# A fused attention and expert kernel: four engines in a new order, LayerNorm's shift on GpSimd, TensorE's program without a loop

## The reference, cut to what matters

```python
# x, ctx: (32, 128, 1024) float32. For each of 32 batches:
a  = layernorm(x, axis=-1)
q  = Wq @ a + bq;  k = Wk @ ctx + bk;  v = Wv @ ctx + bv       # 128 x 1024 each
k, v = pad(k, 8, 7), pad(v, 8, 7)
attn = softmax over a window of 16 keys around each position, 8 heads of 16 channels
x1 = x + Wo @ (attn weights times v) + bo
z  = layernorm(x1, axis=-1)                                   # 128 rows of 1024
w  = softmax(z @ gate_w.T); the top 2 of 8 experts, weights normalised to sum 1
out = x1 + sum over experts e of w[:, e] * ((z @ lora_A[e].T) @ lora_B[e].T)   # rank 64
```

## Time and profile before

| | |
|---|---|
| median of 3 runs | 1264.25 us (1264.19 to 1271.45) |
| the profiled execution | 1263.59 us, of which 1261.8 us are its span |
| PE busy | 1074.9 us, 85% of the span, 24452 matmuls |
| DVE / ACT / POOL busy | 898.5 / 574.4 / 416.9 us |
| mean granted clock of TensorE | 0.916 of full speed |

### The profile page before, as it was taken

One profiled execution on the slowest core, in us unless ns is written; L12 is line 12 of the kernel. 1 busy time (PEld: TensorE's weight loads), 2 busy tenths in 40 slices (PEclk: granted clock), 3 DMA queues, 4 the chain that ended last, 5 costly groups with the idle time before them and its releaser, 6 DMA issues.

```text
span 1261.8 us, 55007 instructions
## 1 busy us (share of the span) xinstructions
PE 1074.9 (85%) x24452; PEld 909.8 (72%) x24452; DVE 898.5 (71%) x1922; ACT 574.4 (46%) x809; POOL 416.9 (33%) x306
## 2 busy tenths in 40 slices
PE   4658898988989888998988989888988888989986
PEld 2547786776778677776776878677876777877875
DVE  3567777776768767777776778777677776778873
ACT  4545535444545444444444444444454444455431
POOL 3563323333323233233333223233233333323220
PEclk8778998889989889988989989989988989989999
DMA  4422233123232123232123232123231232332210
GB/s 169 121 70 53 70 87 80 47 67 87 70 86 72 51 70 86 71 86 66 57 70 87 70 87 66 59 67 87 71 86 42 64 86 71 87 86 69 55 36 34
DMA packets 157313, 92.87 MB, mean 74 GB/s; under 512 B 139680, under 2 KB 139808, under 8 KB 156704
## 3 DMA queue, kind: packets, MB, share of 16 engines
q1 hardware_dynamic: 157088, 89.25, 25.4%
HBM read 55.16 MB, written 16.78 MB: 57 GB/s over the span
## 4 chain that ended last, share of the span: by engine, by line
issue 43%; POOL 20%; PE 16%; DVE 13%; ACT 4%; DMA 2%; SPq 1%; POOLq 0%; DVEq 0%
PE bank_a L310 8%; POOL prob L911 8%; POOL ctx_split L917 5%; PE bank_c L310 3%; POOL x_split L943 3%; PE bank_b L360 3%; POOL attn_split L934 2%; DVE row_max L744 2%; DVE row_sum L758 1%; PE bank_b L339 1%; DMA raw<-x 1%; ACT k_sb L575 1%; DVE prob L750 1%; SPq L246 1%; DVE stats L673 1%
## 5 line engine op out<-in xcount | busy, mean ns | idle before, releaser
L911 POOL TENSOR_TENSOR prob<-prob,row_inv 128x512 f32<-128x512 f32 x128 | 134.4, 1050 | 427.8 <-DVE row_inv L762 426.1
L360 PEld LDWEIGHTS bank_b<-prob_t,v_diag 64*64 64x64 f32 x4608 | 214.3, 148 | 49.2 <-issue 26.2
L360 PE MATMUL bank_b<-prob_t,v_diag 64*64 64x96 f32 (+2 forms) x4608 | 228.8, 257 | 15.4 <-DMA v_diag<-v_t 14.4
L310 PE MATMUL bank_a<-down_split,mid_split 128*128 128x264 f32 (+1 forms) x1536 | 215.9, 289 | 8.5 <-issue 6.8
L310 PEld LDWEIGHTS bank_a<-down_split,mid_split 128*128 128x128 f32 x1536 | 194.8, 189 | 16.5 <-issue 8.6
L769 DVE STREAM_TRANSPOSE prob_t<-prob 128x768 f32<-128x768 f32 x128 | 124.9, 976 | 111.8 <-POOL prob L911 110.6
L310 PE MATMUL bank_a<-up_split,ht_split 128*128 128x512 f32 x768 | 194.3, 402 | 3.5 <-DVE ht_split L859 3.5
L558 ACT ACTIVATE prob<-prob 128x512 f32<-128x512 f32 x128 | 80.8, 631 | 248.5 <-DVE prob L750 248.3
L339 PEld LDWEIGHTS bank_b<-k_sb,q_diag 32*32 32x32 f32 x16384 | 153.4, 104 | 39.5 <-issue 33.3
L339 PE MATMUL bank_b<-k_sb,q_diag 32*32 32x32 f32 x16384 | 169.1, 194 | 9.3 <-issue 6.5
L310 PEld LDWEIGHTS bank_a<-up_split,ht_split 128*128 128x128 f32 x768 | 141.0, 190 | 34.1 <-ACT ht_split L634 3.4
(11 more groups left out here) (76 smaller groups left out, 1360.6 us busy)
## 6 DMA issues: line engine op xcount, KB each, us to landing
v_diag<-v_t SPq DMA_DIRECT2D x128, 132.0 KB
raw<-x SPq DMA_DIRECT2D x32, 512.0 KB, 4.1
resid_pair<-x SPq DMA_DIRECT2D x32, 512.0 KB, 4.4
out<-resid_pair SPq DMA_DIRECT2D x32, 512.0 KB, 2.6
raw<-ctx SPq DMA_DIRECT2D x31, 512.0 KB, 3.6
prob_t<-up_w SPq DMA_DIRECT2D x1, 1024.0 KB, 6.3
resid_pair<-up_w SPq DMA_DIRECT2D x1, 1024.0 KB, 5.7
v_diag<-down_w SPq DMA_DIRECT2D x1, 1024.0 KB, 7.6
```

What stands on the lines that cost most here:

```text
L310: return nc.tensor.matmul(dst, st[:, s, st_cols], mv[:, m, mv_cols], start=start and n == 0, stop=stop and n == 2)
L360: last = nc.tensor.matmul(bank_b[2 + m % 2][rows, lo * PW:hi * PW], value_blocks(b)[rows, n, :], prob_t[rows, at:at + (hi - lo) * KT], sta ...
L911: nc.gpsimd.tensor_tensor(weights_of(m), weights_of(m), row_inv[:, cols].unsqueeze(2).broadcast_to([P, CT, KT]), ALU.mult).then_inc(prob_d ...
```

## The change

It leaves the computation and TensorE's order of work as they are. It changes:

- the order of work inside a step on VectorE, ScalarE, GpSimd and the DMA queue;
- LayerNorm's `shift`, which becomes a second small multiplication on GpSimd behind `rstd`; VectorE prepares -mean by one more `tensor_scalar`;
- TensorE's `steps`, called with `loops=0`: all 36 steps stand written out. The other engines keep their loop;
- `choose_experts`, which is cut in two, with VectorE's work of chunk 2 between the halves; the difference of the two logits goes into ScalarE's exponential, a product becomes a `tensor_scalar`, a sum of two tiles a `tensor_reduce`;
- D0, which waits for the split of each half of the rows apart;
- writing the mask back to the score bank, which becomes an item of its own in ScalarE's order, behind more urgent work.

```diff
-        def steps(eng, step):
-
-            first, tail = 3, 5
-            loops = (BATCHES + 2 - first - tail) // 2
+        def steps(eng, step, loops=(BATCHES + 2 - 3 - 5) // 2):
...
-                    pe.wait_ge(xt_hi, old.count(2, 2))
-                    pe.wait_ge(xt_lo, old.count(2, 2))
+                    pe.wait_ge(xt_hi, old.count(2, 1))
+                    pe.wait_ge(xt_lo, old.count(2, 1))
...
                 if old:
+                    pe.wait_ge(xt_hi, old.count(2, 2))
+                    pe.wait_ge(xt_lo, old.count(2, 2))
                     for f in range(4, FK):
...
-            steps(pe, step)
+            steps(pe, step, loops=0)
...
                 nc.scalar.activation(weights_of(m), weights_of(m), ACT.Exp).then_inc(exp_done, 1)
+
+            def write_mask(cur, m):
+
+                act.wait_ge(shifted, cur.count(CHUNKS, m + 1))
                 nc.scalar.activation(bank_b[m % 2][:], mask[:], ACT.Copy).then_inc(mask_set, 1)
...
+            def gap_exponential(old):
+
+                act.wait_ge(gate_step, old.count(GATE, 6))
+                nc.scalar.activation(gate[:, 1:2], top[:, 0:1], ACT.Exp, bias=top[:, 1:2],
+                                     scale=-1.0).then_inc(gap_exp, 1)
...
-                nc.vector.tensor_scalar(var_eps[:, which:which + 1], moments[:, which, 1:2], EPS, None,
+                nc.vector.tensor_scalar(var_eps[:, which, 0:1], moments[:, which, 1:2], EPS, None,
                                         ALU.add).then_inc(semaphore, 1)
-
-            def layernorm_shift(which, semaphore, batch):
-
-                nc.vector.scalar_tensor_tensor(shift[:, which:which + 1], moments[:, which, 0:1], -1.0,
-                                               rstd[:, which:which + 1], ALU.mult,
-                                               ALU.mult).then_inc(semaphore, 1)
+                nc.vector.tensor_scalar(var_eps[:, which, 1:2], moments[:, which, 0:1], -1.0, None,
+                                        ALU.mult).then_inc(semaphore, 1)
...
-                nc.vector.tensor_tensor(gate[:, 4:5], gate[:, 1:2], gate[:, 3:4], ALU.mult).then_inc(gate_step, 1)
-                dve.wait_ge(gate_step, old.count(13, 10))
+                dve.wait_ge(gate_step, old.count(GATE, 8))
+                nc.vector.tensor_scalar(gate[:, 4:5], gate[:, 1:2], gate[:, 3:4], None,
+                                        ALU.mult).then_inc(gate_step, 1)
+                dve.wait_ge(gate_step, old.count(GATE, 9))
...
+            def rows_norm(which, step_done, ready, b):
+
+                pool.wait_ge(step_done, b.count(6, 6))
+                nc.gpsimd.tensor_tensor(rstd[:, which:which + 1], var_eps[:, which, 0:1], consts[:, 2:3],
+                                        ALU.pow).then_inc(ready[0], 1)
+                pool.wait_ge(ready[0], b.count(1, 1))
+                nc.gpsimd.tensor_tensor(shift[:, which:which + 1], var_eps[:, which, 1:2],
+                                        rstd[:, which:which + 1], ALU.mult).then_inc(ready[1], 1)
```

More of the change, by code:

```diff
@@ L67 @@
 D1 = ER2 + EXPERTS
+GATE = 12
 EPS = 1e-5
@@ L226, in steps @@
                 peeled(i)
-            with eng.Fori(0, loops) as j:
-                for u in range(2):
-                    step(*(Batch(j, first + u + d) for d in (2, 1, 0, -1, -2)))
+            if loops:
+                with eng.Fori(0, loops) as j:
+                    for u in range(2):
+                        step(*(Batch(j, first + u + d) for d in (2, 1, 0, -1, -2)))
             for i in range(first + 2 * loops, BATCHES + 2):
@@ new lines, in normalise_x, with normalise_x1 @@
+            def normalise_x(later):
+                act.wait_ge(shift1, later.count(1, 1))
+                for target in (x_split[:, 0, :], raw[:]):
+                    last = nc.scalar.activation(target, raw[:], ACT.Identity, bias=shift[:, 0:1],
+                                                scale=rstd[:, 0:1])
+                last.then_inc(xn_done, 1)
+            def normalise_x1(old):
+                act.wait_ge(shift2, old.count(1, 1))
+                if old.c == 0:
+                    act.wait_ge(weights_lo, 5)
+                nc.scalar.activation(xn2[:], resid[old.parity], ACT.Identity, bias=shift[:, 1:2],
+                                     scale=rstd[:, 1:2]).then_inc(xn2_done, 1)
@@ L592, in step @@
-                if ahead and ahead.c >= 1:
-                    act.wait_ge(ctx_in, ahead.count(16, 16))
-                    nc.scalar.activation(ctx_split[:, 0, :], ctx_of(ahead), ACT.Copy).then_inc(ctx_hi, 1)
+                    exponentials(cur, 0)
+                    evacuate_v(cur)
+                    write_mask(cur, 0)
+                if ahead:
+                    if ahead.c >= 1:
+                        context_hi(ahead)
+                if old:
+                    rows_hi(old, 0)
+                    rows_hi(old, 1)
@@ L596, in step @@
                 if prev:
                     even_heads(prev, 2)
-                if cur:
-                    exponentials(cur, 1)
+                if ahead and not cur:
+                    evacuate_k(ahead)
                 if ahead:
-                    if not cur:
-                        evacuate_k(ahead)
                     place_q(ahead)
@@ new lines, in residual @@
+            def residual(prev):
+                x1 = resid[prev.parity]
+                dve.wait_ge(resid_in[prev.parity], prev.turn(1))
+                for n in range(2):
+                    half = slice(n * HALF, (n + 1) * HALF)
+                    dve.wait_ge(o_done, prev.count(2, n + 1))
+                    nc.vector.scalar_tensor_tensor(x1[:, half], bank_c[:, half], bias[:, 3:4],
+                                                   x1[:, half], ALU.add,
+                                                   ALU.add).then_inc(x1_done, 1)
@@ L849, in step @@
                 if old:
+                    gate_experts(old)
+                if later:
+                    first_norm(later)
+                if cur:
+                    weights_transpose(cur, 1)
+                if old:
+                    weigh_experts(old, 0)
                     weigh_experts(old, 1)
@@ new lines, in attention_lo, with normal_lo @@
+            def attention_lo(prev):
+                pool.wait_ge(attn_hi, prev.count(1, 1))
+                nc.gpsimd.tensor_tensor(attn_split[:, 1, :], attn[:], attn_split[:, 0, :].bitcast(F32),
+                                        ALU.subtract).then_inc(attn_lo, 1)
+            def normal_lo(later):
+                pool.wait_ge(xn_done, later.count(1, 1))
+                nc.gpsimd.tensor_tensor(x_split[:, 1, :], raw[:], x_split[:, 0, :].bitcast(F32),
+                                        ALU.subtract).then_inc(xn_lo, 1)
@@ L937, in step @@
[L937 to L946 removed]
+                    rows_norm(0, ln1_step, (rstd1, shift1), later)
```

271 lines of the change are left out of this document (120 added, 151 removed).

## The result

The changed kernel takes 1091.07 us (median of 4 runs, 1090.62 to 1096.37), the kernel before in the same comparison 1266.51 (1264.19 to 1271.45). The ratio is 0.862, with a 95% interval of 0.858 to 0.866. Forecast were 1097 and 1066 to 1150, so the prediction holds. Its parts don't all hold.

A forecast was written before the change was run, and what follows sets the result against it. TensorE was taken as bound by its work plus 7.50 us a step of waits (`h_sb`, `k_sb`, issue) and lowered clock. 1263.6 - 166.7 - 2.4 + 3 = 1097.5 us; range 1066 to 1150.

The forecast's parts named there:

- The forecast's case: TensorE loses all its waits for `h_sb` and `k_sb` and the clock's loss: 1097 us, chance 0.70.
- The hand walk: One step timed from V's start: `h_sb` ready at 20.2 to 21.45 us for hT at 21.2, `k_sb` at 21.1 before O.
- The second rival: A new wait replaces the old: VectorE delayed by 2.0 us leaves idle time before hT; 1174 us, chance 0.20.
- the sum: From 1263.6 us, 166.7 saved in 26 steps and 2.4 in another, 3 added in the tail: 1097.5 us.
- the clean step: Step near the end of the kernel before, without work on `later`: 31.66 us, taken as each looped step's new time.
- The head: Before the full steps: later weight splits cost some us, `k_sb` waits go; taken as 0, with 8 to either side.
- the tail: At the end, the split of `attn` waits for the expert choice and the gate for a LayerNorm: +3 us.
- 2.2 us net leave its stream: Shift to GpSimd: VectorE loses 162 ns and 2.34 us a step, gains two `tensor_scalar` of about 0.15, ahead of `h_sb`.
- Of a kind that the row at 1169.35 shows unharmed: VectorE's `tensor_scalar` took 0.15 us under a GpSimd instruction, so `attn_split` would not hold the new one replacing the gate's product.
- I book no gain: Writing out TensorE's program: no gain, as straight code also has issue time, 1.1 us in the clean step.
- the bounds 0.4 to 2.4: TensorE's issue time per step, us: 0.4 with branch stalls gone, 2.4 with two packet-end stalls.
- The fourth rival: Straight code starves TensorE, each of six packets a step coming late: 7.7 us per step, 1269 us; chance 0.05.

The follow-up runs named there:

- run 3: Changed kernel with LayerNorm's shift computed on VectorE again, right behind GpSimd's `rstd`: 1115.3 us, ratio 0.878 to the kernel before.
- runs 10 and 12: Changed kernel with small matmuls added once at the head of TensorE's program: 73 in run 10, 1114.6 us; 52 in run 12, 1078.1 us.
- run 1: Kernel before with only LayerNorm's shift moved to GpSimd, behind `rstd`: 1293.0 us, ratio 1.021.
- run 2: Kernel before with only `attn_split` placed ahead of `rstd` on GpSimd: 1175.8 us, ratio 0.926.
- Run 8: Kernel before with `attn_split` ahead of `rstd`, TensorE written out, x normalised late on ScalarE, and GpSimd's chunk 2 product ahead of `x_split`: 1170.0 us.
- run 9: Changed kernel with TensorE's hardware loop put back: 1122.2 us, ratio 0.882 to the kernel before.
- run 11: Changed kernel with the finished batch's store issued behind the issues of `v_diag` and the next x load: 1093.4 us, ratio 0.861 to the kernel before.

## Why the prediction was right

**Waits and clock.** The forecast's case came out. Both waits are gone, O takes 1.63 us (1.64 was forecast), the granted clock in the steps is 1.00. The hand walk put `h_sb` between 20.2 and 21.45 us, and hT's start at 21.2; in the trace `h_sb` ends 0.05 us before hT starts, and run 3 shows that a further 0.8 us is waited for and gives 1115. The second rival was put at a delay of 2.0 us; it stood much nearer than its 0.20 says, and that the forecast was met to 6 us is in part luck: the hold of `pick`, which the sum did not have, used up the margin and no more, and runs 10 and 12 show that a few small matmuls more at the head of TensorE's program move the time by -13 or +23 us. `k_sb` was in time as walked (557.05 + 1.11 = 558.16, O at 558.58).

**The sum, term by term.** The 26 steps were to save 166.7 us and saved 989.86 - 816.58 = 173.3: a step is 31.41 us, not the clean step's 31.66. The step ahead of the clean one gave 2.0 (2.4 forecast), the clean one itself 0.2 (0). The head cost 1.7 (0), the tail 1.1 (3). 173.3 + 2.0 + 0.2 - 1.7 - 1.1 = 172.7 us, the difference of the spans. The tail's cost was where it was said to be, in the split of `attn` behind the expert choice. O starts 0.10 us behind the end of GpSimd's `attn_split` (1050.99 + 2.34 = 1053.33), after 4.68 us that the profile calls issue; in the kernel before these were 1.55 us, and O took 1.61. Of these 4.4 us more, the rest of the tail gave 3.3 back:

```profile
1053.43 2.90 PE L312 MATMUL bank_c<-attn_split,w_split 128*128 128x512 f32 x6 [4.68 <-issue]
...
1061.01 0.66 PE L371 MATMUL bank_a<-ident,h_sb 128*128 128x128 f32 x4 [1.26 <-DVE h_sb L773]
```

**The shift.** "2.2 us net leave its stream" had the right instruction and the wrong reason. What freed it is GpSimd's order, in the old order at least: alone, moving the shift costs 25 us (run 1), and placing `attn_split` ahead of `rstd` saves 94 (run 2) with the shift where it was. What the move does buy in the new order is a handshake of 0.8 us (run 3). Its cost was sized well: the product on GpSimd takes 0.19 us, within 0 to 1.05.

**The held instruction.** "Of a kind that the row at 1169.35 shows unharmed" failed for `pick`. That row, like 552.25 here, is on 128x1 elements and isn't held; on 128x8 elements the pair takes 1.61 us under `attn_split`, and 0.48 clear of it. The rule of the Trainium skill that I set aside (SBUF — State Buffer, section "SBUF: two separate sides": VectorE in a two-port mode is blocked too) fits the 128x8 pair. The 128x1 row was no ground to set it aside: it speaks for its own shape only, and whether that instruction was in such a mode no run here shows. The prediction gave such a hold the second rival's sum; it cost 1.1 us of VectorE and nothing of TensorE in the step shown, since `h_sb` was still just in time.

**ScalarE.** The prediction named only the passes over x as what stands before `k_sb`. Run 8 shows a second cause behind them, the late subtraction of chunk 2 with the mask's write behind it, which keeps the wait at its size without the passes. The walk was right since it took the subtraction at its new place; of the mask it booked nothing.

**The written-out program.** "I book no gain" was the term most off: taking it back costs 31 us (run 9). The sum came out all the same, because the clean step from which all was measured was itself straight code: its 1.1 us of idle time already lacked the branch, so the gain was inside the 6.41 us a step. The idle time is 0.80 us a step, within the bounds 0.4 to 2.4. Of the Trainium skill's rule (Runtime: NRT & Kernel Launch, section "Instruction fetch mechanics") the first half agrees with run 9, where a pause of 2.4 to 3.0 us stands behind each branch; the second, that fetching is otherwise hidden, doesn't agree with pauses of 0.3 to 1.3 us in straight code, if these are fetches, as their places in runs 10 and 12 suggest. The fourth rival was far off: even with 73 matmuls more the pauses came to 1.3 us a step, not 7.5. The 256 instructions of a packet came out, by the shifts of runs 10 and 12, but not by their working: it took 64 bytes an instruction from the page before, and by the changed page 3.15 MB for 54694 instructions are 57.6.

## What to carry to other kernels

- Moving the instruction that another engine holds did not cure the hold here: it went to what came next. Move the one that holds, to where the other engine's work isn't sensitive.
- The orders of the engines have to be judged together. The same ScalarE order cost 10% alone, nothing with GpSimd's matching order, and stands in the fastest kernel with VectorE's; an edit of one queue that fails alone proves little about it.
- When a clean step of the same kernel is in the trace, take it as the estimate of what a step without waits takes, and say what it includes: here it included the gain of straight code.

## What the runs showed of the hardware

- Which VectorE instruction GpSimd's pass over 128x1024 elements holds depends on its kind and shape: `tensor_scalar` on 128x1 took 0.14 us under it, the pair on 128x8 1.61 us instead of 0.48, a product of two 128x1 tensors 1.79 us instead of 0.16, and two statistics over 512 columns 1.29 us with it (666.04 in run 2) as without it (554.81 in the changed kernel).
- GpSimd takes 0.55 us for a power on 128x1 elements and 0.19 for a product.
- Straight code on TensorE isn't free of pauses, and its time depends on where in the program they fall: 0, 52 or 73 tiny matmuls once at the head of the program make 1091, 1078 or 1115 us. The best number holds for this program alone, since an edit of TensorE's code shifts the places, and so did a moved store (run 11).
